# Softmax denominators of a self-attention: from broadcast products to direct sums with full-bank reciprocals

## The reference

```
q = rope(rms_norm(X @ WQ + bQ));  k = rope(X @ WK + bK);  v = X @ WV + bV
w = (q . k) / |k| * mask[branch]
probs = softmax(concat([w, tanh(sink)]))
out = probs[..., :T] @ v + probs[..., T:] * v_null
y = mean over branches of (out @ WO + bO);  x = x + y
```

## Time and profile before

| | |
|---|---|
| median of 3 runs | 2210.67 us (2207.01 to 2215.05) |
| the profiled execution's own time | 2211.0 us |
| its span, first to last instruction | 2209.2 us |
| busy in the span | PE 1969.3, DVE 1886.3, ACT 1325.0, POOL 1297.0 us |
| mean granted TensorE clock | 0.953 of full |
| self-attention, from the trace | 0 to about 673 us |
| one batch of it, from one output product to the next | 37.2 us in most, up to 39.5 us |

### The profile page before, as it was taken

How to read it: one execution, slowest core, us unless ns; L and a number is a source line. 1 busy time by engine, 2 the same in 40 slices (tenths; PEclk the granted TensorE clock), 3 DMA queues, 4 the chain that set the end, 5 groups by cost and what they waited for, 6 DMA issues and landing times.

```text
span 2209.2 us, 50184 instructions
## 1 busy us (share of the span) xinstructions
PE 1969.3 (89%) x19536; PEld 1531.8 (69%) x19536; DVE 1886.3 (85%) x3501; ACT 1325.0 (60%) x2640; POOL 1297.0 (59%) x1566
## 2 busy tenths in 40 slices
PE   4899999999988889999898998998989989899866
PEld 2566666666563778787787777886878777777753
DVE  6667576767644699999999999999999999999993
ACT  4333333333322577877777778787777777777753
POOL 6465565656443356666656656666565666666542
PEclk8899999999988999999999999999999999999976
DMA  6000000000036010111101101111010110110100
GB/s 199 13 16 21 16 16 21 13 24 13 24 143 145 28 36 14 41 31 36 33 21 53 33 21 41 27 40 33 22 53 19 36 39 21 48 33 22 36 1 12
DMA packets 51175, 82.35 MB, mean 37 GB/s; under 512 B 9809, under 2 KB 26465, under 8 KB 50938
## 3 DMA queue, kind: packets, MB, share of 16 engines
q1 hardware_dynamic: 46442, 71.70, 11.1%
q0 software_dynamic: 2736, 4.16, 1.0%
q10 hardware_dynamic: 1760, 3.28, 0.5%
HBM read 60.54 MB, written 9.86 MB: 32 GB/s over the span
## 4 chain that ended last, share of the span: by engine, by line
DVE 44%; PE 10%; issue 9%; ACT 3%; POOL 1%; DMA 1%; POOLq 0%; DVEq 0%; ACTq 0%; another core or an unknown queue 0%
DVE ca_top L1613 19%; DVE ca_W L1624 17%; DVE ca_W L1621 4%; DVE ca_top L1604 3%; PE ca_pF L88 2%; PE ca_pF L89 2%; PE ca_pF L90 2%; DMA x_scratch<-y_scratch 1%; PE ca_pX L1357 1%; ACT ca_W L1409 1%; PE ca_pT L1255 1%; PE ca_pO L1302 1%; PE ca_pS L88 1%; PE ca_pX L1348 1%; POOL ca_S L1102 0%
## 5 line engine op out<-in xcount | busy, mean ns | idle before, releaser
L1624 DVE MATCH_REPLACE8 ca_W<-ca_top,ca_W 128x722 f32<-128x722 f32 (+1 forms) x624 | 555.1, 899 | 0.0
L1613 DVE MAX8 ca_top<-ca_W 128x8 f32<-128x722 f32 (+1 forms) x624 | 538.5, 903 | 1.7
L1102 POOL TENSOR_TENSOR ca_S<-ca_S,ca_W 128x722 f32<-128x722 f32 (+1 forms) x208 | 357.8, 1740 | 104.5 <-ACT ca_W L1409 104.5
L88 PE MATMUL ca_pS<-ca_KH,ca_QH 128*128 128x362 f32 (+1 forms) x384 | 150.5, 392 | 105.7 <-ACT ca_S L1426 97.8
L1080 POOL TENSOR_TENSOR ca_KL<-ca_K,ca_KH 128x384 fp32r<-128x384 f32 (+1 forms) x128 | 123.0, 961 | 200.8 <-ACT ca_KH L1401 198.3
L1419 ACT ACTIVATE ca_S<-ca_S,ca_shift 128x722 f32<-128x722 f32 (+1 forms) x208 | 175.9, 891 | 54.2 <-POOL ca_shift L1094 54.0
L1409 ACT ACTIVATE ca_W<-ca_W,ca_shift 128x722 f32<-128x722 f32 (+1 forms) x208 | 186.5, 897 | 27.4 <-DVE ca_W L1624 27.2
L341 POOL TENSOR_TENSOR sa_ss<-sa_ss,sa_minus_half 100x16 f32<-100x16 f32 x64 | 190.1, 2986 | 21.2 <-DVE sa_ss L528 21.2
L1431 ACT ACTIVATE ca_PT<-ca_pT 128x768 f32<-128x768 f32 (+1 forms) x208 | 163.0, 784 | 65.4 <-PE ca_pT L1255 61.1
L88 PE MATMUL ca_pF<-ca_cH,ca_WkH 128*128 128x338 f32 (+1 forms) x512 | 188.5, 368 | 9.4 <-ACT ca_K L1399 9.4
L1604 DVE MAX8 ca_top<-ca_S 128x8 f32<-128x722 f32 (+1 forms) x208 | 180.0, 903 | 16.6 <-ACT ca_S L1426 16.2
(11 more groups left out here) (223 smaller groups left out, 5142.1 us busy)
## 6 DMA issues: line engine op xcount, KB each, us to landing
ca_raw<-in_ctxT SPq DMA_DIRECT2D x32, 384.0 KB, 3.7
ca_raw<-in_ctxT SPq DMA_DIRECT2D x32, 338.0 KB, 3.1
ca_RKH<-ca_KH SPq DMA_DIRECT2D x64, 90.2 KB, 2.1
ca_RKL<-ca_KL SPq DMA_DIRECT2D x64, 90.2 KB, 2.1
sa_xin<-in_x SPq DMA_DIRECT2D x16, 200.0 KB
sa_xres<-in_x SPq DMA_DIRECT2D x16, 200.0 KB
x_scratch<-sa_x SPq DMA_DIRECT2D x16, 200.0 KB
x_scratch<-y_scratch POOLq DMA_DIRECT2D x16, 200.0 KB, 13.6
```

What stands on the lines that cost most here:

```text
L88: pe.matmul(out, ah, bh, start=start, stop=False)
L1102: pool.tensor_tensor(S[k][rows, :], S[k][rows, :], W[r][rows, :], ALU.subtract).then_inc(p_ready, 1)
L1613: n_of[t.i] = order.mark(dve.max(top[r][rows, 8 * k:8 * k + 8], W[r][rows, :]))
L1624: ins = dve.match_replace(W[r][rows, :], eight, W[r][rows, :], REMOVED)
```

## The change

The denominator product gets `fours`, a whole 101x32 matrix of fours, in place of `pick`. So each product writes the sum of its own head and branch to all 32 rows of that head, at the place where the spread reciprocals stood before, and the 48 spreading products, their ACT copies, `pick` and `rden` go. The three banks `den_bank` (the former `rb_bank`) are filled branch by branch, 16 denominator products and then 16 numerator products each, at the end of the body. The reciprocal of 128x100 between `rope(1)` and `rope(2)` goes; in the next body, after `low(0)`, DVE takes for each branch the reciprocal of the whole 128x400 bank and multiplies. PE's L690 transposes now wait for all three reciprocals (`den_ready`), because the second denominator bank is `pt`; the denominators wait for `x1_ready`, in body 15 for `out3_ready` too.

The null row is made in place on partitions 96 to 100 (five equal rows; 96 to 99 are overwritten later), so the two moving DMAs go, and five of the setup transfers become broadcasts to five rows. At the start, the setup transfers go ahead of the bias transfers, which now wait for the first four high parts; all 24 low parts are on DVE.

```diff
@@ POOL, start
-            for t, a in BIAS:
-                pool.dma_start(t, a).then_inc(bias_in, 16)
+            for t, a in SETUP:
+                pool.dma_start(t, a).then_inc(setup_in, 16)
...
-                pool.dma_start(V[T:T + 1, :, :].rearrange("p n d -> p (n d)"),
-                               V[0:1, :, :].rearrange("p n d -> p (n d)")).then_inc(null_in, 16)
-                pool.wait_ge(null_weights, 1)
-                pool.dma_start(E[T:T + 1, :, :, :].rearrange("p h n q -> p (h n q)"),
-                               E[0:1, :, :, :].rearrange("p h n q -> p (h n q)")).then_inc(null_in, 16)
...
-                    for t, a in SETUP:
-                        pool.dma_start(t, a).then_inc(setup_in, 16)
+                    pool.wait_ge(hi_made, CC)
+                    for t, a in BIAS:
+                        pool.dma_start(t, a).then_inc(bias_in, 16)
+                    nulls()
@@ ACT
-                if prev:
-
-                    need(act, y_mm, b.count(1, -1))
-                    for n in range(NL):
-                        act.wait_ge(rb_mm, b.count(HK * NL, HK * (n + 1 - NL)))
-                        act.activation(rb[:, n, :], rb_bank[n], ACT.Copy).then_inc(rb_ready, 1)
@@ DVE
                     squares(1)
                     biased(2)
+                    lows(range(QKU, QKU + 2))
                     squares(2)
+                    biased(3)
+                    lows(range(QKU + 2, QKU + CC))
+                    squares(3)
                     rope(0)
-                    biased(3)
-                    squares(3)
+                    lows(range(QKU + CC, len(UNITS)))
+                    rope(1)
                     statistics(1)
-                    rope(1)
...
-                    dve.wait_ge(num_mm, b.count(HK, 0))
+                    need(dve, y_mm, b.count(1, -1))
                     for n in range(NL):
-                        dve.wait_ge(rb_ready, b.count(NL, n + 1 - NL))
+                        dve.wait_ge(den_mm, b.count(NL * HK, HK * (n + 1 - NL)))
+                        dve.reciprocal(rb[:, n, :], den_bank[n]).then_inc(den_ready, 1)
+                        dve.wait_ge(num_mm, b.count(NL * HK, HK * (n + 1 - NL)))
+                        dve.wait_ge(den_ready, b.count(NL, n + 1 - NL))
                         dve.tensor_tensor(rb[:, n, :], pq[:, n, 0:CC * T], rb[:, n, :], ALU.mult).then_inc(num_used, 1)
...
-                if cur:
-                    dve.wait_ge(den_mm, b.count(HK, HK))
-                    dve.reciprocal(rden[:, :], pq[:, 3, 0:T]).then_inc(rden_ready, 1)
@@ PE
-                    for n in range(NL):
-                        for g in range(CC):
-                            for k in range(HK):
-                                rows = slice(DH * k, DH * k + DH)
-                                last = pe.matmul(rb_bank[n][rows, T * g:T * g + T], spread(NL * g + n, k),
-                                                 rden[rows, :], start=True, stop=True)
...
-                    need(pe, rb_ready, b.count(NL, 0))
+                    need(pe, den_ready, b.count(NL, 0))
                     for c in range(CC):
                         last = pe.transpose(pt[:, T * c:T * c + T], xn[:, 128 * c:128 * c + 128], ident[0:T, 0:T])
...
+                    if prev:
+                        pe.wait_ge(x1_ready, b.count(1, 0))
+                    if not nxt:
+                        pe.wait_ge(out3_ready, 1)
+                    for n in range(NL):
+                        for g in range(CC):
+                            for k in range(HK):
+                                last = pe.matmul(den_bank[n][DH * k:DH * k + DH, T * g:T * g + T], fours[:, :],
+                                                 E[0:T + 1, HK * g + k, n, :], start=True, stop=True)
```

More of the change, by code:

```diff
@@ L157, in self_program @@
         bvl = sb("bvl", [128, NL, CC])
-        xin, xn, xres, x1 = (sb(n, [T, D]) for n in ("xin", "xn", "xres", "x1"))
+        xin, xn = sb("xin", [T, D]), sb("xn", [T, D])
+        xres_all, x1_all = sb("xres", [T + 1, D]), sb("x1", [T + 1, D])
+        xres, x1 = xres_all[0:T, :], x1_all[0:T, :]
         stats, mv, rstd = sb("stats", [T, 6]), sb("mv", [T, 2]), sb("rstd", [T, 1])
@@ L202, in self_program @@
         stage = [E[:, :, :, :].rearrange("p h n q -> p (h n q)")[:, piece(u)] for u in range(RING)]
-        row = rb[0:1, :, :].rearrange("p n q -> p (n q)")
-        null_bias = [xres[0:1, :], x1[0:1, :], row[:, 0:D]]
+        null = slice(96, T + 1)
+        NULLS = T + 1 - 96
+        row = rb[null, :, :].rearrange("p n q -> p (n q)")
+        null_bias = [xres_all[null, :], x1_all[null, :], row[:, 0:D]]
         sinks0, tanh0, exp0 = (row[:, D + 64 * n:D + 64 * n + NH * NL] for n in range(3))
@@ L361, in body @@
                         power(n)
[L362 to L366, removed]
                 if far:
@@ L389, in null_exps @@
                 act.wait_ge(sink_steps, 4)
-                act.wait_ge(lo_made, QKU)
-                act.wait_ge(v_lo_made, len(UNITS) - QKU)
+                act.wait_ge(lo_made, len(UNITS))
                 for br in range(NL):
-                    w = exp0[:, NH * br:NH * br + NH].unsqueeze(2).broadcast_to((1, NH, T))
-                    last = act.activation(E[0:1, :, br, :], w, ACT.Copy)
-                last.then_inc(null_weights, 1)
+                    w = exp0[:, NH * br:NH * br + NH].unsqueeze(2).broadcast_to((NULLS, NH, T))
+                    act.activation(E[null, :, br, :], w, ACT.Copy).then_inc(null_weights, 1)
             def body(b, cur, prev, nxt, far):
@@ L459, in lows @@
                                       ALU.subtract).then_inc(lo_made, 1)
[L461 to L465, removed]
             def constants():
@@ L542, in body @@
                     statistics(0)
-                    lows(range(2))
+                    lows(range(1))
                     normalised(0)
+                    lows(range(1, 2))
+                    turned()
                     lows(range(2, CC))
-                    picks()
-                    turned()
                     lows(range(CC, 2 * CC))
@@ L664, in turn @@
                     last.then_inc(hT_mm, 1)
[L666 to L670, removed]
-                    for n in range(NL):
-                        for g in range(CC):
-                            for k in range(HK):
-                                rows = slice(DH * k, DH * k + DH)
-                                last = pe.matmul(rb_bank[n][rows, T * g:T * g + T], spread(NL * g + n, k),
-                                                 rden[rows, :], start=True, stop=True)
-                                if g == CC - 1:
-                                    last.then_inc(rb_mm, 1)
                 if cur:
@@ L695, in body @@
                 if prev:
-                    pe.wait_ge(rb_ready, b.count(NL, 0))
+                    pe.wait_ge(den_ready, b.count(NL, 0))
                     pe.wait_ge(ctx_ready, b.count(1, 0))
@@ L752, in body @@
                     if not prev:
-                        pe.wait_ge(null_in, 32)
-                        pe.wait_ge(pick_ready, 1)
-                    for c in range(CAP):
-                        g, n = divmod(c, NL)
-                        for k in range(HK):
-                            last = pe.matmul(pq[DH * k:DH * k + DH, 3, 0:T], picker(c), E[0:T + 1, HK * g + k, n, :],
-                                             start=c == 0, stop=c == CAP - 1)
-                            if c == CAP - 1:
-                                last.then_inc(den_mm, 1)
@@ L762, in body @@
-                    for c in range(CAP):
-                        g, n = divmod(c, NL)
-                        for k in range(HK):
-                            h = HK * g + k
-                            last = pe.matmul(pq[DH * k:DH * k + DH, n, T * g:T * g + T],
-                                             V[0:T + 1, n, DH * h:DH * h + DH], E[0:T + 1, h, n, :],
-                                             start=True, stop=True)
-                            if c == CAP - 1:
-                                last.then_inc(num_mm, 1)
+                        pe.wait_ge(null_values, NL)
@@ new lines, in body @@
+                        pe.wait_ge(null_weights, NL)
+                        pe.wait_ge(fours_ready, 1)
+                    if prev:
[7 more added lines that the diff above has]
+                                                 E[0:T + 1, HK * g + k, n, :], start=True, stop=True)
+                                if g == CC - 1:
+                                    last.then_inc(den_mm, 1)
+                        for g in range(CC):
+                            for k in range(HK):
+                                h = HK * g + k
+                                last = pe.matmul(pq[DH * k:DH * k + DH, n, T * g:T * g + T],
+                                                 V[0:T + 1, n, DH * h:DH * h + DH], E[0:T + 1, h, n, :],
+                                                 start=True, stop=True)
```

(2 more changed lines are left out.)

48 lines of the change are left out of this document (19 added, 29 removed).

## The result

The changed kernel takes 2336.88 us (median; 2333.89 to 2337.75), beside 2212.86 us of the kernel before on the same chip: a ratio of 1.056 (95% interval 1.054 to 1.059). That is 0.9 us from the 2336 forecast. The difference itself is 124.0 us between these medians and 125.4 us between the profiled spans, where the forecast's sum was 126.

What follows compares the result with a forecast made beforehand. The self-attention was taken as bound by a ring of DVE and PE arcs, 37.2 us a batch. Terms 107.8 + 5.1 + 1.6 + 21.6 - 10 = +126 us gave 2336 us, range 2304 to 2360.

Steps and rivals of the forecast that it cites:

- The reading of the bound: Self-attention batch: a ring of DVE and PE work, 37.2 us together; work added to DVE's arc lengthens it one for one.
- DVE's arc: DVE's unpaused work from biased(3) to the context's last sum, some 19.1 us; the new reciprocals stand in its middle.
- the first rival: DVE's 11 us idle per batch hides the reciprocals, PE bounds and loses 2.1 us per seam: 2167 us; chance 4%.
- The reciprocals: After low(0) on DVE: three of 2.65 us, 8.05 us with hand-over; +7.7 us net per seam, 107.8 over fourteen.
- The rivals at 1.94 and 3.10 us: Time per reciprocal bank: cheap at 1.94 us gives 2304 us (rival's chance 6%); dear at 3.10 gives 2357 (8%).
- the hand-over: Between each wide reciprocal and the product reading its result on DVE: some 0.04 us lost each time.
- the 0.36 from POOL's powers: At rope(3): removing the 0.69 us reciprocal returns only 0.36 us, since rope(3) also waits for POOL's third power.
- The clock: PE's output product at half rate after the pause of over 8 us: 12 more seams at 1.8 us, 21.6 us.
- The last seam's own term: End of self-attention: denominators wait for out3_ready, then three reciprocals and products; last sum 664.3 rather than 662.71, +1.6 us.
- Body 15's: Seam of body 15, already late behind the spreading products: context ready at about 640.0 rather than 634.84, +5.1 us.
- The start: Before batch 0: turn(1) at about 54.6 rather than 64.92, -10 us, bounds -12.5 and -4.
- The likeliest span of 2322 to 2350: Whole kernel: span of the likeliest case, the forecast as summed with the start anywhere in its bounds; chance 66%.

Runs made afterwards that it cites:

- the run with PE kept busy: The changed kernel with ten products of 512 columns added on PE behind turn(1), in its pause, result overwritten unread: 2316.09 us, ratio 1.0465.
- the copy run: The changed kernel with a plain copy of each 128x400 denominator bank in place of its wide reciprocal: 2246.0 us, ratio 1.015.
- the exp run: The changed kernel with 1/d made on ACT as exp(-ln d) and no reciprocal on DVE: 2203.99 us, ratio 0.9966.

## Why the prediction was right, and where only its sum was

**The reading of the bound** held. DVE's arc grew by 7.98 us, the interval with PE at full clock grew by 7.98 us (45.18 against 37.2), and where the reciprocals left the arc the interval fell to 36.91. DVE's idle time in the batch hid nothing, so the first rival fell. The prediction called itself wrong if anything but the last sum released the output product. The row at 430.56 shows no wait, because PE's slow `turn(3)` ends only there; but the product starts 0.15 us after the sum's end, as it did before, and where PE is at full clock the wait for the sum is back (0.63 us at 418.99).

**The reciprocals.** 2.65 us was forecast from the 4-column and the 100-column row, and 2651, 2649 and 2648 ns were measured. The rivals at 1.94 and 3.10 us fell with it, as did the estimate of 3.5 from the Trainium skill (VectorE: DVE Perf Modes, First, the fixed hardware budget): the repeat count of 8 that it gives is no price per column here. What was a little off is the hand-over: a reciprocal is followed by its product after 2.75 us (418.96 to 421.71), not 2.69. So three cost 8.25 rather than 8.05 (the whole stretch grew by 8.29); the 0.36 from POOL's powers was 0.31. In sum +7.98 for a seam against 7.7, some 4 us over fourteen seams.

**The clock** was mis-sized, in the way it was counted. The half rate came in every seam, and the run with PE kept busy puts 20.8 us on it. But that is what the changed kernel pays in all, and the kernel before paid a part already: its mean interval was 37.68 against 37.2 clean. An interval lost 46.65 - 45.18 = 1.47 us to the clock after and 0.48 before; the net, 0.99 x 15, is about 15 us, not 21.6. The slow products last 5.28, 5.76 and 4.31 us in turn, 1.47 us over 3.65 in the mean, where I took 1.8 from three single rows; and before, the slowest of the three slow ones (5.95) stands in the first seam, which so lost nothing more to the clock. The sign that I had named, 5.2 us or more in nearly all seams, held in two of three.

**Where the terms fell.** Of the twelve slow products in the 21.6 us, two (those that start in bodies 14 and 15) stand at the head of the last two intervals, so 3.6 us belong there and 18.0 to bodies 1 to 14. Bodies 1 to 14 then took 123.1 us (6.5 in the first, from `turn(1)` to the output product, and 116.6) where 107.8 + 18.0 = 125.8 was forecast: 4 us more for the reciprocals, 5 less for the clock, and 1.5 less in the first seam. The last two intervals took 8.2 + 3.8 = 12.0 us, where 5.1 + 1.6 + 3.6 = 10.3 was forecast. Their two products take 5.76 and 5.83 us, against 3.65 before, which is 4.3 of the 12.0. The last seam's own term held: 12.9 us from `out3_ready` (776.78) to the last sum (789.66), against 12.4. Body 15's was about 1 us too low.

**The start.** `biased(0)` was held by the bias transfers until 22.98 (forecast 23), the last normalisation came at 53.61 (54.5), but `turn(1)` at 56.63 rather than 54.6: -8.3, not -10. A term was missing: ACT wrote V late enough for PE to pause 2.71 us, and the third branch's values behind it took 6.31 us, mostly at half clock (3.60 in a full seam).

So the errors were -2.7 over bodies 1 to 14, +1.7 on the last two intervals, +1.7 at the start and -1.5 us that no step covers. They cancel to within 1 us. That is partly luck: the single steps were off by 1 to 5 us, and the median of the kernel before alone lies between 2209.85 and 2213.28 us on the chips used here. The likeliest span of 2322 to 2350 was also wider than the terms give; the start's bounds alone make it 2334 to 2343.

## What to carry to other kernels

Before an idle engine is counted as room, look for the ring: which engine's last instruction releases the other's first, and where in the ring the idle time lies. Work removed from the arc where an engine runs beside another buys nothing, and work put into the arc that counts is paid in full, in every round; the same work moved to where that engine waits costs almost nothing. When two halves of a change touch different stages, run each alone: here one is worth 14 us and the other costs 138.

## What the runs showed of the hardware that was not expected

- PE fell to half rate after far less idle time than the 8.5 us pause: with pauses of 1.37, 0.75 and 2.27 us in a seam its output product took 5.67 us in nearly every batch (the copy run), while the new start alone, with 0.64 and 0.63 us ahead of it, took 3.65 in most. One product of 512 columns in the right gap was worth about 22 us over the program.
- The sizes of the pauses don't decide it alone. With 1.37, 0.75, 0.46, 0.47 and 0.63 us in a seam the exp run kept a granted clock of 1.00 from 136 to 616 us. And the kernel before has the same pauses, 0.70 and 0.62 us, ahead of its slow product at 219.70 as ahead of the fast one at 370.28. What decides in such a case these runs don't show.
- A reciprocal on DVE was linear in its columns at the three widths measured, 4, 100 and 400 (6.23 and 6.25 ns a column between them), and took the same from SBUF (2.64 us) as from PSUM (2.65). A copy of the same bank takes 0.56.
- DVE's instructions with two operands of 100 x 256 took 1.5 us instead of 0.42 while POOL worked on tensors of 5 x 512. Whether it is the port that they share was not tried by itself.
- ACT made the three banks' reciprocals as exp(-ln d) in 2.7 us of activations and two table loads of 1.28 us, 5.3 us in all, against DVE's 7.95.
